# Attention and a gated recurrence on one core: the softmax division in the layout of the values product, context stores sent by ScalarE, low parts of x by GpSimd

## The chip, the cores and the metric

The kernel runs on one core of one Trainium2 chip. The metric is the device time of one execution in microseconds (us), lower is better. A core has TensorE (PE, matrix products), VectorE (DVE), ScalarE (ACT), GpSimd (POOL) and SyncE (SP, which only issues transfers), each with its own instruction stream; they wait for each other through semaphores.

## The reference

Sixteen sequences of 512 tokens with 256 features. Sliding-window attention with 16 heads of width 16, then a layernorm, then a recurrence over the sequences whose state feeds three gates, then a second layernorm.

```python
qkv = jnp.einsum('bse,fe->bsf', x, w_in)
scores = jnp.where(valid, qb @ k2.T * scale + slopes * delta, -jnp.inf)   # own block of 128 keys and the one before
out = softmax(scores) @ v2                                                 # per head, D = 16
x = layernorm(x + out @ w_out.T)                                           # attention half
ft, it = sigmoid(xt @ wf.T + c @ uf.T + bf), sigmoid(xt @ wi.T + c @ ui.T + bi)
gt = tanh(xt @ wc.T + c @ uc.T + bc)
c = ft * c + it * gt                                                       # scanned over the 16 sequences
h = tanh(x @ wo.T + c_final @ uo.T + bo)
x = layernorm(x + h)
```

## The kernel before

Every fp32 operand of a product is kept as a high and a low part ("hi" and "lo": the value rounded, and the rest), and each product is three passes over them (`PASSES`). ACT writes the high part with a Copy, DVE (or POOL) subtracts it for the low part.

The main loop has 16 iterations, and each engine has its own `iteration(t)` with its order written out by hand. One iteration is cut into 16 slots, `attend(0)` to `attend(15)`. In a slot PE computes raw scores of sequence t for two heads (`raw_scores`, L940), DVE takes their row maxima (`maxima`, L689), and PE computes the final scores of the slot seven places back (`scores`, L961), of which ACT takes the exponential (`exps`, L448) and POOL clears what lies outside the window (`window`, L347 and L349). A PSUM bank of raw scores is written again only when DVE has read it, one slot later (`red_done`), and one of final scores only when ACT has read it (`exp_done`). Between the slots stand the other products: of sequence t+1 the queries and keys (`project_qk`, `qk_halves`), of t the values (`v_halves`), of t-1 the product of probabilities and values (`values`, L975), of t-2 the output projection (`out_halves`), of t-3 and t-2 the gates (`gate_halves`). Halves of 64 rows run side by side under L921.

The path that the change touches: `values(t-1, g)` gives, for four heads, a bank with 32 rows per head: 16 rows of contexts, the denominator in row 16 (the value matrix has a column of ones), tokens along the free axis. ACT copies it to `ctx_raw` (`ctx_out`, L459), PE transposes it in four blocks (`ctx_transpose`, L983), DVE takes reciprocals of the denominators (L698) and multiplies them into `o_tok` (L703, both in `normalise`). In the next iteration PE transposes `o_tok` back in eight blocks (`o_transpose`, L1016), ACT and DVE make `oT`'s two parts (`ot_hi`, `ot_lo`), and `project_out` or `out_halves` multiplies by `Wout`. `x_hi` (ACT, L426) and `x_lo` (DVE, under L661, where a helper stands for all low parts) split the transposed input of the next sequence, from `xt_raw`. `update` (L736, L738, L740) makes the new state, and `c_hi`, `c_lo` (POOL, L364) split it.

SP issues transfers in one order: `parts_to_dram` and `stack` bring queries and keys through DRAM into stacked layout, `max_to_stack` adds the row of maxima, and the loads of `xt_raw` and `x_res` and the store of `y` lie between. After the loop `last_sequences` finishes the sequences in flight, and a second phase computes the tanh and the second layernorm for all sequences.

## Time and profile before

| | |
|---|---|
| time, three runs | 1002.41, 1003.2, 1004.5 us; median 1003.2 |
| profiled execution | 1004.63 us, of which its instructions span 1002.9 us |
| PE busy | 915.2 us, 91% of the span, 9500 matmuls |
| DVE busy | 719.0 us, 72% |
| ACT busy | 575.9 us, 57% |
| POOL busy | 407.6 us, 41% |
| granted TensorE clock, mean | 0.953 of full |
| DMA, main queue | 129.95 MB, 44.2% of 16 engines |

Busy means that an instruction was in execution; matmuls overlap each other, so a busy PE is an engine that issues without a gap, not one at its peak. An engine's idle time is named with what ended it. The span has a start until about 27 us, the 16 iterations, the last sequences from about 829 us, and the second phase from about 906 us.

### The profile page before, as it was taken

What the parts mean: (1) busy time and instruction counts of PE and PEld (TensorE: products, weight loads), DVE (VectorE), ACT (ScalarE), POOL (GpSimd) and SP (SyncE); (2) the same over time, 40 slices, a digit from 0 to 9 for tenths busy, and PEclk for the clock granted to TensorE, in tenths of its full rate; (3) what the DMA queues carried; (4) which work ended last, traced back from release to release, by engine and by line L of the source; (5) the groups of instructions that cost most, each with busy time, mean ns of one, the idle gap of its engine ahead of it and who ended that gap; (6) DMA issues with size and microseconds to landing.
All of it is one profiled execution on the core that took longest, in us unless ns stands there. A gap on an engine that the chain in (4) does not pass through costs nothing.

```text
span 1002.9 us, 25924 instructions
## 1 busy us (share of the span) xinstructions
PE 915.2 (91%) x9500; PEld 753.2 (75%) x9500; DVE 719.0 (72%) x2795; ACT 575.9 (57%) x1167; POOL 407.6 (41%) x687
## 2 busy tenths in 40 slices
PE   3587879999999999999999999999999989889994
PEld 2375668878788878788878787878787867668884
DVE  7766576877777777777777778787878673327885
ACT  5144556555656565656565656565756464325886
POOL 5142443354444444444444444444444353101443
PEclk9577889999999999999999999999999999899998
DMA  7634443535454545444544454444444400121764
GB/s 257 168 117 121 129 140 126 151 120 143 135 140 137 138 138 139 139 137 139 134 143 133 144 129 146 129 147 129 146 108 145 124 28 22 42 91 49 221 202 132
DMA packets 93534, 131.86 MB, mean 131 GB/s; under 512 B 12128, under 2 KB 47584, under 8 KB 93408
## 3 DMA queue, kind: packets, MB, share of 16 engines
q1 hardware_dynamic: 93136, 129.95, 44.2%
q8 instruction: 76, 1.25, 0.5%
q14 instruction: 50, 0.41, 0.1%
q10 hardware_dynamic: 272, 0.26, 0.1%
HBM read 79.31 MB, written 50.33 MB: 129 GB/s over the span
## 4 chain that ended last, share of the span: by engine, by line
PE 64%; DVE 25%; ACT 5%; issue 4%; POOL 2%; DMA 0%; ACTq 0%; DVEq 0%; POOLq 0%
PE bank L921 29%; DVE bank L689 11%; PE bank L909 11%; PE bank L940 8%; PE bank L975 7%; PE bank L961 3%; DVE max_q L689 3%; DVE qk_parts L661 2%; PE bank L983 2%; DVE gate L738 2%; DVE gate L736 1%; PE bank L1016 1%; PE bank L1029 1%; ACT Pt L643 1%; DVE stats L877 1%
## 5 line engine op out<-in xcount | busy, mean ns | idle before, releaser
L689 DVE CUSTOM_DVE_ANT_0 bank<-bank,mask 128x256 f32<-128x256 f32 (+1 forms) x1024 | 369.3, 423 | 136.1 <-PE bank L940 134.5
L448 ACT ACTIVATE Pt<-bank 128x512 f32<-128x512 f32 (+1 forms) x512 | 248.2, 536 | 204.1 <-PE bank L961 204.0
L347 POOL TENSOR_SCALAR_AFFINE_SELECT Pt<-Pt 128x512 f32<-128x512 f32 x256 | 174.7, 682 | 414.8 <-ACT Pt L448 414.8
L940 PE MATMUL bank<-Ks,Qs 59*128 59x256 f32 (+1 forms) x1024 | 149.5, 320 | 51.3 <-DVE max_q L689 40.5
L940 PEld LDWEIGHTS bank<-Ks,Qs 59*128 59x128 f32 x1024 | 108.5, 192 | 94.8 <-DVE max_q L689 54.5
L689 DVE DVE_READ_ACCUMULATOR2_ANT max_q<- 128x1 f32 x1024 | 144.6, 141 | 0.0
L349 POOL TENSOR_SCALAR_AFFINE_SELECT Pt<-Pt 128x384 f32<-128x384 f32 x256 | 139.3, 544 | 0.0
L975 PE MATMUL bank<-Pt,Vp 128*32 128x256 f32 (+1 forms) x2048 | 131.2, 377 | 0.0
L921 PE MATMUL bank<-x1T,Wg 64*128 64x512 f32 x960 | 128.0, 398 | 0.8 <-DVE o_tok L703 0.8
L921 PE MATMUL bank<-cT,Ug 64*128 64x512 f32 x960 | 125.8, 393 | 0.0
L961 PE MATMUL bank<-Qs,Ks 60*128 60x256 f32 (+1 forms) x1024 | 112.1, 271 | 0.4 <-ACT Pt L448 0.3
L975 PEld LDWEIGHTS bank<-Pt,Vp 128*32 128x32 f32 x2048 | 81.5, 116 | 32.1 <-issue 8.2
L921 PEld LDWEIGHTS bank<-cT,Ug 64*128 64x128 f32 x960 | 89.6, 184 | 17.7
L921 PEld LDWEIGHTS bank<-x1T,Wg 64*128 64x128 f32 x960 | 87.4, 185 | 18.6 <-DVE o_tok L703 0.9
L961 PEld LDWEIGHTS bank<-Qs,Ks 60*128 60x128 f32 x1024 | 95.7, 193 | 2.3 <-issue 1.3
L486 ACT ACTIVATE gate<-bank,bias_half 128x512 f32<-128x512 f32 x64 | 42.5, 687 | 44.7 <-PE bank L921 23.9
L459 ACT ACTIVATE ctx_raw<-bank 128x512 f32<-128x512 f32 x64 | 38.2, 597 | 49.7 <-PE bank L983 47.6
L909 PE MATMUL bank<-xT,Win 128*128 128x512 f32 x204 | 55.5, 425 | 8.6 <-DVE Win L661 8.6
L921 PE MATMUL bank<-Win,xT 64*128 64x256 f32 x768 | 56.7, 291 | 0.0
L909 PEld LDWEIGHTS bank<-xT,Win 128*128 128x128 f32 x204 | 40.5, 205 | 17.6 <-DVE Win L661 8.6
L921 PEld LDWEIGHTS bank<-Win,xT 64*128 64x128 f32 x768 | 52.8, 197 | 0.0
L661 DVE SCALAR_TENSOR_TENSOR qk_parts<-bank,qk_parts 128x512 fp32r<-128x512 f32 x64 | 42.6, 686 | 14.2 <-ACT qk_parts L431 14.2
(111 smaller groups left out, 1345.7 us busy)
## 6 DMA issues: line engine op xcount, KB each, us to landing
parts_dram<-qk_parts SPq DMA_DIRECT2D x128, 256.0 KB
Qs<-parts_dram SPq DMA_DIRECT2D x128, 128.0 KB, 2.6
Ks<-parts_dram SPq DMA_DIRECT2D x128, 128.0 KB, 2.7
xt_raw<-in_xt SPq DMA_DIRECT2D x16, 512.0 KB, 4.2
Qs<-parts_dram SPq DMA_DIRECT2D x128, 64.0 KB, 2.6
Ks<-parts_dram SPq DMA_DIRECT2D x128, 64.0 KB, 2.7
x_res<-in_x SPq DMA_DIRECT2D x16, 512.0 KB, 3.9
x_dram<-y SPq DMA_DIRECT2D x16, 512.0 KB, 3.7
```

Source lines behind the costliest of these rows:

```text
L347: gp.affine_select(out=p4[:, :, 0:128], in_=p4[:, :, 0:128], compare_op=ALU.is_ge, fill=0.0, base=0, pattern=[[0, 4], [1, 128]], channel_m ...
L349: gp.affine_select(out=p4[:, 0:3, 128:256], in_=p4[:, 0:3, 128:256], compare_op=ALU.is_ge, fill=0.0, base=0, pattern=[[0, 3], [-1, 128]], ...
L448: sc.activation(probabilities(g, 2 * pair + odd)[:, S * a:S * a + n], SC[odd][:, 0:n], ACT.Exp).then_inc(exp_done, 1)
L459: sc.activation(ctx_raw[:, :], bank[:, :], ACT.Copy).then_inc(ctx_done, 1)
L486: ins = sc.activation(gate[:, k if k == 3 else which, :], bank[:, :], ACT.Tanh, bias=bias_half[:, which, j:j + 1], scale=0.5)
L661: return ve.scalar_tensor_tensor(out_, in_, scale, hi.bitcast(F32), op0=ALU.mult, op1=ALU.subtract)
L689: ins = ve.tensor_tensor_reduce(out=raw, in0=raw, in1=mask[:, keys], scale=1.0, scalar=MASKED, op0=ALU.add, op1=ALU.max, accum_out=max_q[: ...
L909: ins = te.matmul(out_, w, m, start=(first and n == 0), stop=(last and n == len(todo) - 1))
L921: ins = te.matmul(out_, w(r), m(r), start=(turn == 0 and opens and n == 0), stop=final, skip_group_check=True)
L940: ins = te.matmul(MX[odd][:, 256 * (n % 2):256 * (n % 2) + 256][:, keys], Qs[rows, 2 * g + pair, n * WIN:(n + 1) * WIN], Ks[rows, 2 * g + ...
L961: ins = te.matmul(SC[odd][:, 256 * (j % 2):256 * (j % 2) + width], Ks[rows, 2 * g + pair, j * WIN:(j + 1) * WIN], Qs[rows, 2 * g + pair, j ...
L975: ins = te.matmul(bank[32 * hh:32 * hh + 32, j * WIN:j * WIN + width], Vp[:, j, PITCH * h:PITCH * h + 32], probabilities(g, hh)[:, 256 * j ...
```

## The change

The division by the softmax denominator moves. For sequences 0 to 14 ACT copies each values bank to `ctx_raw` as before, and then sends it itself to `ctx_dram` (one transfer of 256 KB for each g, four per sequence). SP loads the 256 context rows from there to `o_un`, already in the layout that `oT` needs, in two transfers (`load_contexts`), and the 16 denominator rows in pieces of 128 tokens to `den_q` (`load_denominators`, four transfers). DVE transposes them in blocks of 32 (`turn_denominators`), takes the reciprocal of 64 columns (`invert_denominators`) and transposes them back (`turn_inverses`). SP stores them to `inv_dram` (`store_inverses`) and loads them again with every row repeated for the 16 rows of its head (`spread_inverses`, two transfers of 256 KB). POOL multiplies (`scale_contexts`), and ACT and DVE split the result (`ot_hi`, `ot_lo`, now from SBUF). PE's transposes and DVE's `normalise` stay for the last sequence alone.

Besides: the low parts of x are POOL's from sequence 2 on, and their high parts are made two sequences ahead, in slots 11 and 12; `update` is cut in `forget` and `take_in`, and `forget` stands earlier; `stack(t, 2)` goes ahead of the load of `xt_raw`; `Wo` and `Uo` are no longer loaded and split at the start but in the last sequences (`load_last_weights`, `last_weights_hi`), into `Win`'s space.

```diff
-        Wo = sb("Wo", [128, 2, KC, E], F32R)
-        Uo = sb("Uo", [128, 2, KC, E], F32R)
...
+        o_un = sb("o_un", [128, KC, S])
+        inv_den = sb("inv_den", [128, KC, S])
+        den_q = sb("den_q", [128, 128])
+        den_t = sb("den_t", [128, 128])
+        last_o_tok = sb("last_o_tok", [128, NB, E])
...
+        Wo, Uo = Win[:, :, :, 0:E], Win[:, :, :, E:2 * E]
+        out_stage = xt_raw[:, :, :]
...
+        ctx_dram = nc.dram_tensor("ctx_dram", [2, QUADS, 128, S], F32).ap()
+        inv_dram = nc.dram_tensor("inv_dram", [2, 32, S], F32).ap()
...
+            def load_denominators(t):
+
+                sp.wait_ge(den_cleared, 1)
+                for g in range(QUADS):
+                    wait(sp, ctx_stored[g], 16, t, 16)
+                wait(sp, inv_stored, 16, t - 1, 16)
+                rows = ctx_dram[t % 2].rearrange("g (h r) (q i) -> q (g h) r i", r=2 * D, i=128)[:, :, D, :]
+                for q in range(4):
+                    sp.dma_start(den_q[32 * q:32 * q + H, :], rows[q]).then_inc(den_in, 16)
+
+            def load_contexts(t, c):
+                for g in (2 * c, 2 * c + 1):
+                    wait(sp, ctx_stored[g], 16, t, 16)
+                wait(sp, otlo_done, 2, t - 1, c + 1)
+                rows = ctx_dram[t % 2, 2 * c:2 * c + 2].rearrange("g (h r) s -> (g h) r s", r=2 * D)[:, 0:D, :]
+                sp.dma_start(o_un[:, c, :], rows).then_inc(o_un_in[c], 16)
+
+            def store_inverses(t):
+                wait(sp, inv_turned, 1, t, 1)
+                sp.dma_start(inv_dram[t % 2].rearrange("r (q i) -> q r i", i=128), den_q[:, :]).then_inc(inv_stored, 16)
+
+            def spread_inverses(t):
+
+                wait(sp, inv_stored, 16, t, 16)
+                for c in range(KC):
+                    wait(sp, scaled_done, 2, t - 1, c + 1)
+                    rows = inv_dram[t % 2, 8 * c:8 * c + 8]
+                    sp.dma_start(inv_den[:, c, :], rows.unsqueeze(1).to_broadcast([8, D, S])).then_inc(inv_in[c], 16)
+
+            def load_last_weights():
+
+                sp.wait_ge(xlo_done, 2 * B)
+                for n, w in enumerate((w_o, u_o)):
+                    sp.dma_start(out_stage[:, n, :].rearrange("p (c n) -> p c n", c=KC), w.rearrange(v, p=128)).then_inc(last_weights_in, 16)
...
+                if now: stack(t, 2)
+                if by_rows: load_contexts(t - 1, 0)
                 if real(t + 2): load_xt(t + 2)
                 if now:
-                    stack(t, 2)
...
                 if n1: stack(t + 1, 0)
+                if by_rows:
+                    load_denominators(t - 1)
+                    load_contexts(t - 1, 1)
                 if now: max_to_stack(t, 2)
                 if n1: parts_to_dram(t + 1, 1)
+                if by_rows:
+                    store_inverses(t - 1)
+                    spread_inverses(t - 1)
+                if t == B - 1: load_last_weights()
...
+            def x_lo(t, c):
+                wait(pool, xhi_done, 2, t, c + 1)
+                gp.tensor_tensor(xT[:, t % 2, 1, c, :], xt_raw[:, c, :], xT[:, t % 2, 0, c, :].bitcast(F32), ALU.subtract).then_inc(xlo_done, 1)
+
+            def scale_contexts(t, c):
+
+                wait(pool, o_un_in[c], 16, t, 16)
+                wait(pool, inv_in[c], 16, t, 16)
+                gp.tensor_tensor(o_un[:, c, :], o_un[:, c, :], inv_den[:, c, :], ALU.mult).then_inc(scaled_done, 1)
...
+                if p2 and t - 2 < B - 1:
+                    for c in range(KC):
+                        scale_contexts(t - 2, c)
...
+                    if real(t + 2):
+                        for c in range(KC):
+                            x_lo(t + 2, c)
...
-                wait(act, ct_ready, 4, t, g)
+                pt, pg = before(t, g)
+                if pt < B - 1:
+                    wait(act, ctx_stored[pg], 16, pt, 16)
+                else:
+                    act.wait_ge(ct_ready, g)
                 sc.activation(ctx_raw[:, :], bank[:, :], ACT.Copy).then_inc(ctx_done, 1)
-
-            def ot_hi(t, c, bank):
+                if t < B - 1:
+                    wait(act, ctx_done, 4, t, g + 1)
+                    sc.dma_start(ctx_dram[t % 2, g], ctx_raw[:, :]).then_inc(ctx_stored[g], 16)
+
+            def ot_hi(t, c):
                 if c == 0:
                     wait(act, op_ready, 2, t - 1, 2)
-                wait(act, ot_ready, 2, t, c + 1)
+                wait(act, scaled_done, 2, t, c + 1)
+                sc.activation(oT[:, 0, c, :], o_un[:, c, :], ACT.Copy).then_inc(othi_done, 1)
...
+            def last_weights_hi():
+
+                act.wait_ge(last_weights_in, 32)
+                act.wait_ge(v_ready, 2 * B)
+                sc.activation(out_stage[:, 1, :], out_stage[:, 1, :], ACT.Copy, scale=0.5).then_inc(u_o_halved, 1)
+                sc.activation(Wo[:, 0, :, :], out_stage[:, 0, :].rearrange("p (c n) -> p c n", c=KC), ACT.Copy).then_inc(last_hi, 1)
...
-                    ot_hi(t - 2, 0, B0)
-                    ot_hi(t - 2, 1, B1)
-                attend(1)
-                if n1: x_hi(t + 1, 0)
+                    ot_hi(t - 2, 0)
+                    ot_hi(t - 2, 1)
                 attend(2)
-                if n1: x_hi(t + 1, 1)
+                if t == 0: x_hi(1, 1)
...
                 v_out(t, 0, A0)
+                if real(t + 2): x_hi(t + 2, 0)
                 attend(12)
                 v_out(t, 1, A1)
+                if real(t + 2): x_hi(t + 2, 1)
...
+                last_weights_hi()
                 c_hi(t - 2, 0)
...
-            act.wait_ge(weights_in, 80)
-            for n in range(5):
+            act.wait_ge(weights_in, 48)
+            for n in range(3):
...
+            def turn_denominators(t):
+
+                wait(dve, den_in, 64, t, 64)
+                ve.transpose(den_t[:, :], den_q[:, :]).then_inc(den_turned, 1)
+
+            def invert_denominators(t):
+                wait(dve, den_turned, 1, t, 1)
+                own = den_t[:, :].rearrange("p (b r) -> p b r", r=32)[:, :, 0:H]
+                ve.reciprocal(own, own).then_inc(den_inverted, 1)
+
+            def turn_inverses(t):
+                wait(dve, den_inverted, 1, t, 1)
+                ve.transpose(den_q[:, :], den_t[:, :]).then_inc(inv_turned, 1)
+
+            def ot_lo(t, c):
+                wait(dve, othi_done, 2, t, c + 1)
+                minus_hi(oT[:, 1, c, :], o_un[:, c, :], oT[:, 0, c, :]).then_inc(otlo_done, 1)
+
...
-                if p1: normalise(t - 1, 0, A0)
+                if p3: forget(t - 3, 0)
+                attend(1)
+                if t == 0: x_lo(1, 0)
+                attend(2)
+                if t == 0: x_lo(1, 1)
                 if p2:
-                    ot_lo(t - 2, 0, B0)
-                    ot_lo(t - 2, 1, B1)
-                attend(1)
-                if n1: x_lo(t + 1, 0)
-                attend(2)
-                if n1: x_lo(t + 1, 1)
...
-                if p1: normalise(t - 1, 3, A0)
-                if p2:
-                    x1_lo(t - 2, 0, B0)
-                    x1_lo(t - 2, 1, B1)
+                if p1: turn_denominators(t - 1)
+                if p2: x1_lo(t - 2, 0, B0)
+                if p1: invert_denominators(t - 1)
+                if p2: x1_lo(t - 2, 1, B1)
+                if p1: turn_inverses(t - 1)
...
-                    wait(pe, maxrow_done, 4, t - 1, 4)
-                    ctx_transpose(t - 1, 0, A0)
-                if p2:
-                    wait(pe, gate_done, 6, t - 3, 1)
-                    o_transpose(t - 2, 0, B0)
-                    freed(pe, (gate_done, 6, t - 3, 2), (ctx_done, 4, t - 1, 1))
...
-                    wait(pe, o_done, 4, t - 1, 1)
+                    wait(pe, maxrow_done, 4, t - 1, 4)
...
                     o0, o1 = out_halves(0, B0), out_halves(1, B1)
+                    freed(pe, (gate_done, 6, t - 3, 1), (maxrow_done, 4, t - 1, 3))
+                    freed(pe, (gate_done, 6, t - 3, 2), (ctx_done, 4, t - 1, 1))
                     wait(pe, otlo_done, 2, t - 2, 2)
...
-                    wait(pe, maxrow_done, 4, t, 1)
-                    ctx_transpose(t - 1, 1, A0)```

What stands in PE's order behind `values(t-1, 1)` at the start of an iteration, before. L1016 is `o_transpose`, L940 and L961 are slot 1.

```order
L975 MATMUL bank<-Pt,Vp 32x256 x12
L975 MATMUL bank<-Pt,Vp 32x128 x4
L983 MATMUL bank<-ident,ctx_raw 128x128 x4
L1016 MATMUL bank<-ident,o_tok 128x128 x8
L940 MATMUL bank<-Ks,Qs 128x256 x4
L961 MATMUL bank<-Qs,Ks 128x256 x4
L921 MATMUL bank<-x1T,Wg 128x512 x12
```

The same place in the changed kernel (L1106 is `values`, L1071 and L1092 the raw and the final scores):

```order
L1106 MATMUL bank<-Pt,Vp 32x256 x12
L1106 MATMUL bank<-Pt,Vp 32x128 x4
L1071 MATMUL bank<-Ks,Qs 128x256 x4
L1092 MATMUL bank<-Qs,Ks 128x256 x4
L1052 MATMUL bank<-x1T,Wg 128x512 x12
```

The twelve transposes between the values product and slot 1 are gone, and nothing takes their place on PE.

ACT's order in slots 12 to 14, before, from the copy of the first half of the values of sequence t (L438, `v_out`) to the exponentials of slot 14 (L448), with `qk_hi` (L431), `ctx_out` (L459) and `x1_hi` (L477) between:

```order
L438 ACTIVATE Vp<-bank 128x2x16x16
L448 ACTIVATE Pt<-bank 128x384 x2
L438 ACTIVATE Vp<-bank 128x2x16x16
L431 ACTIVATE qk_parts<-bank 128x512
L454 ACTIVATE max_rows<-bank 16x128
L448 ACTIVATE Pt<-bank 128x512 x2
L431 ACTIVATE qk_parts<-bank 128x512
L459 ACTIVATE ctx_raw<-bank 128x512
L477 ACTIVATE x1T<-bank 128x512 x2
L448 ACTIVATE Pt<-bank 128x384 x2
```

And in the changed kernel (L517 is `v_out`, L505 `x_hi`, L527 `exps`, L510 `qk_hi`, L542 and L545 `ctx_out` and its transfer, L578 `x1_hi`):

```order
L517 ACTIVATE Vp<-bank 128x2x16x16
L505 ACTIVATE xT<-xt_raw 128x512
L527 ACTIVATE Pt<-bank 128x384 x2
L517 ACTIVATE Vp<-bank 128x2x16x16
L505 ACTIVATE xT<-xt_raw 128x512
L510 ACTIVATE qk_parts<-bank 128x512
L533 ACTIVATE max_rows<-bank 16x128
L527 ACTIVATE Pt<-bank 128x512 x2
L510 ACTIVATE qk_parts<-bank 128x512
L542 ACTIVATE ctx_raw<-bank 128x512
L545 DMA ctx_dram<-ctx_raw 128x512
L578 ACTIVATE x1T<-bank 128x512 x2
```

The two high parts of x stand between the copies and `qk_hi` now, and a transfer stands between `ctx_out` and `x1_hi`.

SP's order at an iteration's end, before: the last rows of `stack(t+1, 0)`, then `max_to_stack(t, 2)`, `parts_to_dram(t+1, 1)` and, of the next iteration, `max_to_stack(t, 3)` and the first of `stack(t+1, 1)`.

```order
L254 DMA Ks<-parts_dram 32x2x512
L262 DMA Qs<-max_rows 1x8x128 x2
L239 DMA parts_dram<-qk_parts 8x16x512 x4
L262 DMA Qs<-max_rows 1x8x128 x2
L254 DMA Qs<-parts_dram 32x2x512
```

And in the changed kernel:

```order
L267 DMA Ks<-parts_dram 32x2x512
L286 DMA den_q<-ctx_dram 16x128 x4
L293 DMA o_un<-ctx_dram 128x1x512
L275 DMA Qs<-max_rows 1x8x128 x2
L252 DMA parts_dram<-qk_parts 8x16x512 x4
L297 DMA inv_dram<-den_q 4x32x128
L305 DMA inv_den<-inv_dram 128x1x512 x2
L275 DMA Qs<-max_rows 1x8x128 x2
L267 DMA Qs<-parts_dram 32x2x512
```

Eight transfers came in, and the last three of them wait for DVE and for a store to land, ahead of `max_to_stack` and `stack` of the next iteration.

## Rows read from the trace of the kernel before

**Rows 1.** The page: the chain that ended last, by engine.

```profile
PE 64%; DVE 25%; ACT 5%; issue 4%; POOL 2%; DMA 0%; ACTq 0%; DVEq 0%; POOLq 0%
```

**Rows 2.** Windows: us, busy of PE, PEld, DVE, ACT, POOL, clock, DMA, GB/s.

```profile
127.00:178.00 51.00, 46.33 (x500) 37.45 (x501) 36.44 (x165) 28.32 (x59) 19.42 (x36) 0.90 0.45 135
431.00:482.00 51.00, 49.96 (x580) 41.67 (x578) 39.50 (x167) 31.44 (x65) 22.73 (x38) 1.00 0.47 137
```

**Rows 3.** Timeline of PE, one iteration: start, us; idle before in brackets.

```profile
425.20 0.39 PE L940 MATMUL bank<-Ks,Qs 59*128 59x128 f32 x4
...
427.54 0.66 PE L983 MATMUL bank<-ident,ctx_raw 128*128 128x128 f32 x4
428.04 1.04 PE L1016 MATMUL bank<-ident,o_tok 128*128 128x128 f32 x8
429.00 0.50 PE L940 MATMUL bank<-Ks,Qs 59*128 59x256 f32 x4
...
436.31 1.58 PE L921 MATMUL bank<-Wout,oT 64*128 64x256 f32 x24
...
442.43 0.66 PE L983 MATMUL bank<-ident,ctx_raw 128*128 128x128 f32 x4
442.84 3.02 PE L909 MATMUL bank<-xT,Win 128*128 128x512 f32 x12
...
454.78 0.66 PE L983 MATMUL bank<-ident,ctx_raw 128*128 128x128 f32 x4
455.37 0.50 PE L940 MATMUL bank<-Ks,Qs 59*128 59x256 f32 x4
...
458.04 0.32 PE L940 MATMUL bank<-Ks,Qs 59*128 59x128 f32 x1 [0.50 <-DVE max_q L689]
458.80 0.49 PE L940 MATMUL bank<-Ks,Qs 59*128 59x128 f32 x3 [0.44 <-DVE max_q L689]
...
467.29 0.66 PE L983 MATMUL bank<-ident,ctx_raw 128*128 128x128 f32 x4
467.78 1.35 PE L1029 MATMUL bank<-ident,y 128*128 128x128 f32 x8
...
475.70 0.41 PE L940 MATMUL bank<-Ks,Qs 59*128 59x128 f32 x4
```

**Rows 4.** Groups by line: busy us, mean ns | idle before, releaser.

```profile
L364 POOL TENSOR_TENSOR cT<-c,cT 128x512 fp32r<-128x512 f32 x26 | 32.7, 1275 | 0.0
...
L703 DVE TENSOR_TENSOR o_tok<-bank,rden 128x256 f32<-128x256 f32 x64 | 27.2, 425 | 12.0 <-PE bank L1016 10.3
...
L661 DVE SCALAR_TENSOR_TENSOR xT<-xt_raw,xT 128x512 fp32r<-128x512 f32 x32 | 23.3, 730 | 7.1 <-ACT xT L426 6.9
...
L698 DVE RECIPROCAL rden<-bank 128x16 f32<-128x16 f32 x64 | 15.9, 248 | 42.6 <-PE bank L983 42.6
```

**Rows 5.** Timeline of ACT at slot 12 of that iteration.

```profile
465.01 0.60 ACT L431 ACTIVATE qk_parts<-bank 128x512 fp32r<-128x512 f32 x1 [0.16 <-PE bank L921]
```

**Rows 6.** Timeline of the start: ACT's transfer, DVE, POOL.

```profile
0.79 0.47 ACTq L600 DMA_DIRECT2D Pt<-in_w_in  x1
...
24.78 5.57 DVE L661 SCALAR_TENSOR_TENSOR cT<-c,cT 128x512 fp32r<-128x512 f32 x2 [1.16 <-ACT cT L613]
...
28.09 1.71 POOL L340 TENSOR_TENSOR Uo<-ctx_raw,Uo 128x512 fp32r<-128x512 f32 x1
...
30.27 0.29 DVE L689 CUSTOM_DVE_ANT_0 bank<-bank,mask 128x128 f32<-128x128 f32 x1
```

**Rows 7.** DMAs from or to `parts_dram` by tile: time to landing.

```profile
DMA to landing us min/median/max: 2.0/2.7/5.1
```

**Rows 8.** Timeline of SP's queue at an iteration's end.

```profile
467.65 3.33 SPq L239 DMA_DIRECT2D parts_dram<-qk_parts  x4
```

**Rows 9.** Timeline of PE in the last sequences; the wait for a layernorm.

```profile
857.25 1.94 PE L1029 MATMUL bank<-ident,y 128*128 128x128 f32 x8 [3.99 <-ACT y L470]
```

**Rows 10.** Groups by line: one high part of a weight, on ACT.

```profile
L416 ACT ACTIVATE Uo<-ctx_raw 128x512 fp32r<-128x512 f32 x1 | 0.6, 631 | 0.0
```

More of the change, by code:

```diff
@@ L776, in iteration @@
                     qk_lo(t + 1, 1, B1)
+                if p3: forget(t - 3, 1)
                 attend(7)
[L778 removed]
+                if p3: take_in(t - 3, 0)
                 attend(8)
[L780 to L781 removed]
+                if p3: take_in(t - 3, 1)
                 attend(9)
@@ L798, in last_sequences @@
                 (A0, A1), (B0, B1) = pairs_of(B)
-                normalise(t, 0, A0)
-                ot_lo(t - 1, 0, B0)
-                ot_lo(t - 1, 1, B1)
+                last_normalise(0, A0)
+                ot_lo(t - 1, 0)
+                ot_lo(t - 1, 1)
                 residual(t - 1, 0, B0)
@@ L814, in last_sequences @@
                 x1_lo(t - 1, 1, B1)
-                normalise(t, 3, MX[0])
+                last_normalise(3, MX[0])
                 update(t - 1, 0)
-                ot_lo(t, 0, MX[0])
-                ot_lo(t, 1, MX[1])
+                last_ot_lo(0, MX[0])
+                last_ot_lo(1, MX[1])
                 update(t - 1, 1)
@@ L978, in values, with last_ctx_transpose @@
                 ins.then_inc(pv_ready, 1)
-            def ctx_transpose(t, g, bank):
-                wait(pe, ctx_done, 4, t, g + 1)
+            def last_ctx_transpose(g, bank):
+                wait(pe, ctx_done, 4, B - 1, g + 1)
                 for n in range(NB):
@@ L1011, in project_qk, with last_o_transpose @@
                                      for c in range(KC)], qk_ready)
-            def o_transpose(t, c, bank):
-                wait(pe, o_done, 4, t, 4)
+            def last_o_transpose(c, bank):
+                pe.wait_ge(o_done, 4)
                 for n in range(NB):
-                    ins = te.transpose(bank[:, WIN * n:WIN * (n + 1)], o_tok[:, n, 128 * c:128 * c + 128], ident[:, :])
+                    ins = te.transpose(bank[:, WIN * n:WIN * (n + 1)], last_o_tok[:, n, 128 * c:128 * c + 128], ident[:, :])
                 ins.then_inc(ot_ready, 1)
```

143 lines of the change are left out of this document (79 added, 64 removed).

## The prediction

> **What bounds the kernel now.** I read the chain that ended last first: 64% of it is PE and 25% DVE [rows 1]. Then the windows by stage: in the steady part PE is busy 49.96 us of 51 at the full clock, DVE 39.50, ACT 31.44, POOL 22.73, and the DMA engines 0.47 [rows 2]. So there PE issues almost without a gap, and every instruction taken from its stream should shorten the iteration. Two sequences in, from 127 to 178 us, PE is busy 46.33 of 51 [rows 2]; the rest are waits for DVE's maxima. Last I read PE's timeline of one whole iteration, from 425.20 to 475.70, so 50.50 us [rows 3]. Its two idle times over 0.25 us, 0.50 and 0.44, end with DVE's maxima in slot 10 [rows 3].
>
> **What is removed from PE.** A matmul's own length (0.27 to 0.4 us) is no price, since matmuls overlap; the step from the first of a group to the next group is. The transposes of `ctx_raw` at 427.54 take 0.50 until `o_transpose` starts, `o_transpose` 0.96 until slot 1, and the other three groups 0.41, 0.59 and 0.49 [rows 3]. Sum 2.95 us per iteration. Nothing comes in on PE.
>
> **What leaves DVE, and where it waits.** Four `normalise` at 0.248 + 0.425 = 0.67 us are 2.7 us, two low parts of x at 0.73 are 1.5 [rows 4]. In slots 7 to 10, where PE waited 0.94 us for it, DVE loses one `normalise` and has both `forget` instructions earlier (0.7 each, by the row of the same size [rows 4]): 2.0 us less work against 0.59 us less on PE before it. I take the whole 0.94 as gained; the bounds are 0 and 0.94. With it the iteration could fall by 3.89 us.
>
> **What comes in on DVE.** Two block transposes of 128 columns and a reciprocal of 64 columns stand in no trace of before. A transpose costs between 0.248 (16 columns) and 0.73 (512 columns) [rows 4]; I take 0.35, since 128 columns are nearer the first. The Trainium skill (VectorE: DVE Perf Modes, The three transpose paths) gives 311 ns for 128x128 in bf16; by it the sum would be the same. The reciprocal lies between 0.248 and four times that, 0.99; I take 0.6. Together 1.3 us (0.75 to 2.45), in slot 13, where DVE waits for the high parts of x1 anyway. Cover gone, they would delay the maxima of slot 14.
>
> **What comes in on ACT, and the give-back in slots 12 to 15.** ACT has idle time enough in sum, but `qk_hi` of slot 12 waited only 0.16 us for PE [rows 5], and two high parts of x, 0.63 us each by the row of one of the same size [rows 10], now stand ahead of it. Behind it wait DVE's low part, then the maxima of slot 13, then the second low part, then the bank into which PE transposes x1. The delay is between 0 and 1.26 - 0.16 = 1.10; I take 0.6, since the exponentials between had some idle time of their own. The transfer that ACT issues behind `ctx_out` costs its queue 0.47 us [rows 6], four times an iteration; in slot 13 it stands ahead of the high parts of x1, for which PE's gates wait: 0 to 0.47, I take 0.3. At slots 1, 5 and 10 PE arrives 1.5 us or more earlier at a bank that ACT or DVE must first empty: I take 0.4 for all (0 to 0.8). Given back: 1.3 us (0 to 2.4).
>
> **POOL.** Two low parts of x and two scalings at 1.275 us [rows 4] make its 22.7 us 27.8 of about 48. `values(t, 0)` and `values(t-1, 2)` wait for its windows; both have more than 1.5 us of room by my reckoning, so 0.
>
> **The long path.** From the end of slot 13's low parts: DVE's three instructions and the two low parts of x1 between them, 1.3 + 1.4 us; a store; when it has landed, two loads; two scalings, 2.55; ACT's and DVE's parts, in their places behind slots 1 and 2. A transfer takes 2.0 to 5.1 us to land, median 2.7 [rows 7]. PE has its x1 transposes 42.6 us after the iteration's start [rows 3], which becomes about 40; so the inverses leave DVE at about 43, land in DRAM at 45.7, are spread at 48.9, which is 1.0 us into the next iteration (period 47.9), and are multiplied in at 3.6. ACT takes them at 4.6 to 5.9 and DVE at 7.8 to 9.1. PE's output projection stands 11.11 us into the iteration [rows 3], 9.65 when 1.46 us are gone. Up to ACT's step there is room of about 3.5 us. SP is free in time: `parts_to_dram` holds it for 3.33 us [rows 8] until about 42.5.
>
> **Start and end.** The first maximum is at 30.27, right behind two DVE low parts that took 5.57 us beside POOL's low parts of weights, the last of which is `Uo`'s, 1.71 us until 29.80 [rows 6]. Two of POOL's five low parts and three of ACT's high parts go. I take 2.3 us (0 to 3.4, twice 1.71). At the end ACT makes three high parts of 0.63 us [rows 10] just ahead of the layernorm for which PE waits 3.99 us already [rows 9]: 1.9 us lost. Eight transposes, 0.96 [rows 3], go from PE there, but they hid a `normalise`; I take 0.6. Net loss 1.3.
>
> **The sum.** Iterations 3 to 15: 13 times (3.89 - 1.3 = 2.6), 33.8 us. Iterations 1 and 2: PE idle 4.7 us of 51 [rows 2], DVE relieved by 4.2 - 1.3 and PE by 3 or less; I take 4.2 each (2.6 to 6), 8.4. Start 2.3, end -1.3. In all 43.2. The profiled execution took 1004.6 us for a span of 1002.9; it becomes 959.7 and 961.4. The median of the three runs stands 1.4 lower, at 1003.2, so 960.
>
> **The rivals.**
> (a) Nothing is given back: 3.89 an iteration, and 943. For it: PE was the only engine without idle time. Against it: the 0.16 us of ACT.
> (b) POOL and DVE hold each other up. The two DVE low parts of 5.57 us for 2, against 0.73 for one elsewhere, ran beside POOL's two-input work [rows 4, 6]: such a pair costs DVE about 2 us more each. Four more POOL instructions of 1.275 us come in, and `ot_lo` now reads two SBUF operands, `forget` too. If two of these pairs an iteration fall on DVE instructions that PE waits for, at 1.0 us each, the gain falls by 2 us an iteration: 986. Against it: most DVE work reads PSUM, and DVE idles 11.5 us of 51 [rows 2]. The Trainium skill (SBUF — State Buffer, Who interferes with whom) says that a VectorE instruction with two SBUF inputs and a GpSimd instruction that reads SBUF exclude each other for the whole instruction; by that rule, the trace at 24.78 us agrees.
> (c) The long path comes late and PE stops in slot 3. Both hops at the longest landing, 5.1 twice instead of 2.7 twice, eat 4.8 us against 3.5 of room: 1.3 late, 13 times, 977.
> (d) The same, and slower than before: at 43.2 / 13 = 3.3 us of lateness an iteration nothing is left, which needs hops of 12 us for the two. Then SP, which sits in that wait, also brings `stack` late. At 4 us late: 1012. Against it: the longest landing is 5.1 [rows 7]; for it: 2.1 MB more per iteration (four stores and four loads of 256 KB) on top of 6.9 (137 GB/s [rows 2] over 50.5 us), small rows, and SP's order is full.
> (e) The bound passes wholly to ACT or DVE at once and the time stays: 1003. I see no row for it, as both are idle for a fifth of the time or more.
>
> **How the numbers follow.** Likeliest, 943 to 978 (gains of 3.9 to 1.6 us an iteration, with the ends' bounds; (a) and (c) are its edges): 0.68. Better than 943: 0.04. (b), 978 to 994: 0.13. A late path short of undoing the gain, 994 to 1001: 0.04. (e): 0.02. (d): 0.09. The range 944 to 990 leaves out not quite 2 in 10. Faster by over 0.2%, about what a measurement tells here, 0.89; within it 0.02; slower 0.09.
>
> **What would show it.** Period of iterations from 50.5 to about 47.9; PE without L983 and L1016 rows until the last sequences; no wait of over 0.3 us of PE for DVE in slot 10; new short waits of PE in slots 12 to 14, with DVE's low parts waiting for ACT's `qk_hi`; `scale_contexts` ending about 4 us into an iteration; PE's wait for the layernorm near the end at about 5.9. Wrong would be: a wait of PE at the output projection, which would be the long path; DVE's `ot_lo`, `forget` or transposes of over 1 us each, which would be (b); a period under 47.

## The result

Four runs of the changed kernel took 1042.02, 1044.45, 1050.46 and 1051.42 us, median 1047.45; four of the kernel before on the same chip 1003.85. The ratio is 1.043, with a 95% interval of 1.037 to 1.049. It is slower, where 960 was forecast. The profiled execution took 1042.02 us for a span of 1040.3.

The page of the profile after gives busy time by engine:

```profile
PE 895.3 (86%) x9140; PEld 742.6 (71%) x9140; DVE 684.8 (66%) x2693; ACT 576.1 (55%) x1167; POOL 479.9 (46%) x745
```

PE has 360 matmuls less and DVE 34 us less work, as planned, and yet the span grew by 37.4 us. The windows of the stages of [rows 2], after (same columns):

```profile
127.00:178.00 51.00, 41.43 (x451) 32.94 (x448) 31.84 (x143) 26.70 (x56) 24.52 (x40) 0.83 0.75 174
431.00:482.00 51.00, 47.76 (x545) 40.31 (x537) 36.28 (x156) 30.57 (x64) 27.18 (x43) 0.97 0.66 179
```

No engine has taken PE's place: PE, DVE and ACT idle more in both stretches, and POOL, the one with more work, is busy for only about half of them. That is the mark of waits in a ring of engines and not of a new bound. The view of waits names them (who waited, for what: us in total, times, longest):

```profile
POOL o_un L432 <- DMA inv_den<-inv_dram: 173.8, 30, 11.4
ACT oT L551 <- POOL o_un L432: 88.1, 29, 4.4
...
PE bank L1092 <- ACT Pt L527: 41.2, 15, 5.6
```

Read from the bottom: PE stops once in every sequence for an exponential of ACT (L527), because its bank of scores isn't read yet. ACT is not busy then; it stands in `ot_hi` (L551) for GpSimd's product, and GpSimd stands for the spread of the inverses. The timeline of one such passage starts on SP's queue (start, us to issue, what, how many):

```profile
539.26 4.80 SPq L252 DMA_DIRECT2D parts_dram<-qk_parts  x4
544.11 1.44 SPq L297 DMA_DIRECT2D inv_dram<-den_q  x1
550.33 1.29 SPq L305 DMA_DIRECT2D inv_den<-inv_dram  x2
551.66 0.68 SPq L275 DMA_DIRECT2D Qs<-max_rows  x1
```

VectorE's last transpose of the inverses began at 541.41 and took 0.30, but SP was issuing `parts_to_dram` until 544.06. The store of 64 KB then took until 550.33 to land, 6.2 us, read from the issue of the spread, for which SP waits until the store has landed. All that time SP stood still, the row maxima behind it too. GpSimd, ACT and PE in the same passage (in brackets the idle time before, and what ended it):

```profile
554.28 1.29 POOL L432 TENSOR_TENSOR o_un<-o_un,inv_den 128x512 f32<-128x512 f32 x1 [10.77 <-DMA inv_den<-inv_dram]
```
```profile
555.66 0.63 ACT L551 ACTIVATE oT<-o_un 128x512 fp32r<-128x512 f32 x1 [4.37 <-POOL o_un L432]
558.17 0.63 ACT L551 ACTIVATE oT<-o_un 128x512 fp32r<-128x512 f32 x1 [1.88 <-POOL o_un L432]
558.71 0.85 ACT L527 ACTIVATE Pt<-bank 128x384 f32<-128x384 f32 x2
```
```profile
559.33 0.79 PE L1092 MATMUL bank<-Qs,Ks 60*128 60x256 f32 x4 [2.81 <-ACT Pt L527]
559.89 1.68 PE L1052 MATMUL bank<-Wout,oT 64*128 64x256 f32 x24
```

The exponentials of slot 2 are ready work, queued behind `ot_hi`. From the end of VectorE's transpose to the first multiplication lie 12.6 us.

One iteration later the wait is longer, and it costs twice, in idle time and in clock. PE's timeline, then its windows (stretch, length, busy, granted clock, DMA share, GB/s):

```profile
613.14 1.08 PE L1092 MATMUL bank<-Qs,Ks 60*128 60x256 f32 x4 [4.35 <-ACT Pt L527]
613.81 2.97 PE L1052 MATMUL bank<-Wout,oT 64*128 64x256 f32 x24
```
```profile
607.00:611.00 4.00, 1.79 (x18) 1.00 1.07 144
611.00:615.00 4.00, 1.86 (x15) 0.71 1.10 185
615.00:619.00 4.00, 4.00 (x42) 0.50 1.12 150
619.00:623.00 4.00, 3.89 (x56) 0.94 0.83 161
```

After 4.35 us of idleness the granted clock is at 0.50, the 1.2 GHz level, and the same 24 matmuls that took 1.68 us above take 2.97.

### The profile page after: what moved, and what is told of

Its sections match the earlier page's. It is cut to its first block and busy times, and to the rows that moved or that the text cites. A ratio compares the mean times of both kernels' runs of the same rounds, so it can differ in the third digit from the quotient of the medians.

```text
span 1040.3 us, 25344 instructions
## 1 busy us (share of the span) xinstructions
PE 895.3 (86%) x9140; PEld 742.6 (71%) x9140; DVE 684.8 (66%) x2693; ACT 576.1 (55%) x1167; POOL 479.9 (46%) x745
## 5 line engine op out<-in xcount | busy, mean ns | idle before, releaser
L527 ACT ACTIVATE Pt<-bank 128x512 f32<-128x512 f32 (+1 forms) x512 | 248.0, 536 | 166.2 <-PE bank L1092 164.8
L1071 PE MATMUL bank<-Ks,Qs 59*128 59x256 f32 (+1 forms) x1024 | 145.7, 322 | 45.8 <-DVE max_q L793 28.0
L1071 PEld LDWEIGHTS bank<-Ks,Qs 59*128 59x128 f32 x1024 | 109.6, 199 | 83.9 <-DVE max_q L793 36.9
L1092 PE MATMUL bank<-Qs,Ks 60*128 60x256 f32 (+1 forms) x1024 | 120.2, 285 | 48.1 <-ACT Pt L527 41.2
L1092 PEld LDWEIGHTS bank<-Qs,Ks 60*128 60x128 f32 x1024 | 99.5, 200 | 56.3 <-issue 42.7
L1106 PE MATMUL bank<-Pt,Vp 128*32 128x256 f32 (+1 forms) x2048 | 131.7, 378 | 0.0
L1052 PE MATMUL bank<-x1T,Wg 64*128 64x512 f32 x960 | 128.6, 398 | 2.3 <-ACT ctx_raw L542 2.3
L1052 PE MATMUL bank<-cT,Ug 64*128 64x512 f32 x960 | 126.7, 393 | 0.0
L432 POOL TENSOR_TENSOR o_un<-o_un,inv_den 128x512 f32<-128x512 f32 x30 | 40.0, 1333 | 173.8 <-DMA inv_den<-inv_dram 173.8
L1106 PEld LDWEIGHTS bank<-Pt,Vp 128*32 128x32 f32 x2048 | 81.6, 116 | 32.2 <-issue 8.2
L1052 PEld LDWEIGHTS bank<-x1T,Wg 64*128 64x128 f32 x960 | 91.8, 185 | 17.4 <-issue 4.7
L1052 PEld LDWEIGHTS bank<-cT,Ug 64*128 64x128 f32 x960 | 94.5, 185 | 13.0
L551 ACT ACTIVATE oT<-o_un 128x512 fp32r<-128x512 f32 x30 | 18.9, 631 | 88.1 <-POOL o_un L432 88.1
L1052 PE MATMUL bank<-Wout,oT 64*128 64x256 f32 x672 | 61.7, 337 | 0.0
L765 DVE SCALAR_TENSOR_TENSOR oT<-o_un,oT 128x512 fp32r<-128x512 f32 x30 | 25.1, 836 | 51.0 <-ACT oT L551 50.8
L1052 PEld LDWEIGHTS bank<-Wout,oT 64*128 64x128 f32 x672 | 57.4, 244 | 0.0
```

What stands on the lines that cost most here:

```text
L432: gp.tensor_tensor(o_un[:, c, :], o_un[:, c, :], inv_den[:, c, :], ALU.mult).then_inc(scaled_done, 1)
L527: sc.activation(probabilities(g, 2 * pair + odd)[:, S * a:S * a + n], SC[odd][:, 0:n], ACT.Exp).then_inc(exp_done, 1)
L765: return ve.scalar_tensor_tensor(out_, in_, scale, hi.bitcast(F32), op0=ALU.mult, op1=ALU.subtract)
L1052: ins = te.matmul(out_, w(r), m(r), start=(turn == 0 and opens and n == 0), stop=final, skip_group_check=True)
L1071: ins = te.matmul(MX[odd][:, 256 * (n % 2):256 * (n % 2) + 256][:, keys], Qs[rows, 2 * g + pair, n * WIN:(n + 1) * WIN], Ks[rows, 2 * g + ...
L1092: ins = te.matmul(SC[odd][:, 256 * (j % 2):256 * (j % 2) + width], Ks[rows, 2 * g + pair, j * WIN:(j + 1) * WIN], Qs[rows, 2 * g + pair, j ...
```

## The experiments

The two theories. **The late path**: the inverses' two hops through DRAM end too late, and ready work stands behind the waits for them. **Traffic**: 2.1 MB more an iteration slow every transfer that PE's operands come by. Times of the kernel before were 1003 to 1005 us in every set.

### The division left out

```
 SP:   load_denominators, store_inverses, spread_inverses removed
 POOL: scale_contexts removed
 DVE:  turn_denominators, invert_denominators, turn_inverses removed
-                wait(act, scaled_done, 2, t, c + 1)
+                wait(act, o_un_in[c], 16, t, 16)
```

> The changed kernel with the division of sequences 0 to 14 left out (no denominators read, no transposes and reciprocal on VectorE, no store and spread of the inverses, no scaling on GpSimd); the contexts still go through DRAM and the high part waits for their load alone. Theory 1 (the path of the inverses is late, and ScalarE, GpSimd and SyncE stand waiting for it): the waits of PE for the exponentials (1 to 5.6 us an iteration) go, periods of 48 to 49 us, 955 to 975 us in all. Theory 2 (the 2 MB more of traffic an iteration slow every transfer): three quarters of that traffic are still there, so 1020 us or more.

Measured 978.64 us, ratio 0.976 (0.974 to 0.977), 4 us above the range of theory 1 and far from that of theory 2. Of PE's waits for an exponential one of 0.6 us is left in its view of waits. Traffic is refuted as the main cause: three quarters of it are in this kernel. PE's windows over the 13 sequences from the fourth on, of the kernel before, of the changed one and of this one:

```profile
171.00:829.00 658.00, 640.60 (x7404) 0.99 0.46 131
```
```profile
175.00:864.00 689.00, 624.43 (x7091) 0.97 0.67 167
```
```profile
171.00:804.00 633.00, 604.04 (x7100) 0.99 0.62 169
```

Here PE's busy time falls by 36.6 us against before, 2.8 a sequence, near the 2.95 of the prediction. In the changed kernel it fell by 16.2 only, and PE idled 64.6 us instead of 17.4. So of the 56 us between the last two windows, 35.6 are more idle time and 20.4 are the same matmuls taking longer. The rows show one cause of these, the clock: a mean of 0.97 over 689 us, with 1 and 0.5 as the levels, is some 41 us at the low one, which loses half of them; 0.99 over 633 us is 13. By this estimate the clock accounts for some 14 of the 20.4, with an error of several us, since the column has two digits. It isn't the only thing that changes the busy time: the kernel with the direct way, further down, has 0.99 too and 9.5 us more of it than this one, for which no run shows a cause.

### The transfers alone, in the kernel before

```
+                if t < B - 1:
+                    wait(act, ctx_done, 4, t, g + 1)
+                    sc.dma_start(ctx_dram[t % 2, g], ctx_raw[:, :]).then_inc(ctx_stored[g], 16)
 SP:   the loads, the store and the spreads at the changed kernel's places, into tiles nobody reads;
       the store doesn't wait for DVE, and the spread reads the inverses stored an iteration earlier
```

> The kernel before (division in the context transposes, as it was) with the last weights loaded late to make room, and with the changed kernel's transfers added at the same places in the queues, their data read by nobody: four context stores by ScalarE, two context loads, four denominator loads, the inverse store and two spreads an iteration. Theory 1: nothing waits for them, so 1000 to 1012 us. Theory 2: 1025 us or more, with Qs and Ks landing in 3.5 us instead of 2.6.

Measured 1012.35 us, ratio 1.008 (1.006 to 1.011), at the upper edge of theory 1. So the traffic costs something, and with the late weights it is worth 9 us and not 44: an iteration of the steady part takes 50.9 us instead of 50.5. What this kernel lacks is SP's wait for DVE and for the store of the same iteration. The landings of transfers from or to `parts_dram` rose from 2.0/2.7/5.1 [rows 7] to 2.1/3.0/7.5, yet PE waited only 5 us more for keys in all (15.1 against 10.0) and 2.6 for row maxima.

### The inverses ahead of the parts

```
+                if by_rows:
+                    store_inverses(t - 1)
+                    spread_inverses(t - 1)
                 if n1: parts_to_dram(t + 1, 1)
-                if by_rows:
-                    store_inverses(t - 1)
-                    spread_inverses(t - 1)
```

> The changed kernel with the store of the inverses and their spread issued by SyncE ahead of the 1 MB of projection parts instead of behind it; all work is kept. Theory 1 with the queue as the cause of the lateness: the store issues at once, lands about 2.5 to 3 us later instead of 6.2, the spread lands some 6 us earlier, and the waits of PE for the exponentials go: 970 to 1000 us. Theory 2 (traffic): the same bytes, so 1035 to 1050. If the parts, now later, are waited for by the stacks instead, it stays above 1003 with PE waiting on the loads of Qs and Ks.

Measured 1030.43 us, ratio 1.028 (1.024 to 1.031). SP's queue, and PE's waits:

```profile
529.79 0.56 SPq L297 DMA_DIRECT2D inv_dram<-den_q  x1
532.37 1.27 SPq L305 DMA_DIRECT2D inv_den<-inv_dram  x2
533.76 4.35 SPq L252 DMA_DIRECT2D parts_dram<-qk_parts  x4
538.15 3.59 SPq L275 DMA_DIRECT2D Qs<-max_rows  x2
```
```profile
PE bank L1092 <- DMA Qs<-max_rows: 31.7, 24, 3.2
...
PE bank L1071 <- DMA Ks<-parts_dram: 27.3, 14, 10.9
```

The store now lands in 2.6 us instead of 6.2, and of PE's waits for an exponential one of 0.6 us is left. But SP waits for VectorE and for the store ahead of the parts, and then row maxima and keys come late. Of the 27.3 us for keys, 10.9 are one wait at the start, where the kernel before has one of 10.0. The third outcome named in the expectation came true, and the forecast of 970 to 1000 did not: the lateness had only changed its place.

### Store and spread by ScalarE's queue

```
                 attend(14)
+                if p1: store_inverses(t - 1)
                 attend(15)
+                if p1: spread_inverses(t - 1)
```

> The changed kernel with the store and the spread of the inverses issued by ScalarE, on its own DMA queue (store after slot 14, spread after slot 15), so that SyncE waits for neither and the store isn't behind the 1 MB of parts. With the store in front on SyncE's queue the waits of PE only moved from the exponentials to the loads of row maxima and keys (1030 us). Theory 1, refined (it is the in-order wait for the store, wherever it stands, that costs): both waits go, 978 to 992 us, close to the 979 without any division. If ScalarE's own wait for the store and its 2.5 us of issues hold the gates and exponentials back: 995 to 1015. If traffic or the clock is what is left: above 1020.

Measured 1046.95 us, ratio 1.042 (1.037 to 1.048): no gain at all. The expectation had a time above 1020 for the case that traffic or the clock is what is left; the rows show late hops and waits for them. SP first, then ACT, then PE's wait for the exponentials:

```profile
542.16 4.46 SPq L252 DMA_DIRECT2D parts_dram<-qk_parts  x4
```
```profile
545.65 0.57 ACTq L540 DMA_DIRECT2D inv_dram<-den_q  x1
...
552.89 1.22 ACTq L548 DMA_DIRECT2D inv_den<-inv_dram  x2
554.21 1.26 ACT L584 ACTIVATE gate<-bank,bias_half 128x512 f32<-128x512 f32 x2 [5.32 <-issue]
```
```profile
PE bank L1091 <- ACT Pt L512: 39.6, 15, 4.8
```

The store took 7.2 us, though it wasn't on SP's queue. In the run above it took 2.6, and there too ScalarE had sent a context store of 256 KB 3.0 us before it; what that run lacked was the 1 MB of parts handed over at the same time. So leaving SP's queue doesn't make the store early. What the two late stores share is the parts on the DMA engines, which both queues use. The Trainium skill (DMA: Bandwidth & Descriptors, Issuing engines are not separate DMA queues) says this: transfers run on the same 16 DMA engines and interleave, whichever engine started them. These rows agree. And now ACT stood 5.32 us in front of its gates, so that PE still waited for exponentials, 39.6 us against 41.2 in the changed kernel.

### The way shortened and begun earlier

ScalarE sends each quad's four rows of denominators straight from `ctx_raw` into `den_q`, in which the flat order makes 16 partitions of 128 of them. VectorE inverts all 64 partitions at once. The store is then of 32 KB and no longer of 64, since the unused rows of `den_q` fall away. SP stores behind `stack(t + 1, 0)` and spreads ahead of the parts. All work is kept.

```
+                    sc.dma_start(den_q[16 * g:16 * g + 16, :], ctx_raw[D:128:2 * D, :]).then_inc(den_in, 16)
                     sc.dma_start(ctx_dram[t % 2, g], ctx_raw[:, :]).then_inc(ctx_stored[g], 16)
...
+                ve.reciprocal(den_t[0:64, :], den_q[0:64, :]).then_inc(den_inverted, 1)
...
                 if n1: stack(t + 1, 0)
                 if by_rows:
-                    load_denominators(t - 1)
+                    store_inverses(t - 1)
                     load_contexts(t - 1, 1)
                 if now: max_to_stack(t, 2)
+                if by_rows: spread_inverses(t - 1)
                 if n1: parts_to_dram(t + 1, 1)
```

> The changed kernel, all work kept, with a shorter way for the inverses that starts earlier: ScalarE sends each quad's four rows of denominators straight from its SBUF tile to the tile of denominators (one small transfer beside each context store), VectorE inverts them in one operation of 64 partitions behind slot 11 (no transposes), and SyncE stores and spreads them ahead of the 1 MB of parts. So far: a store ahead of the parts lands in 2.5 us, one behind them in 6.6 us on either queue, and what costs is that PE's work waits for it. Theory: the spread lands before slot 15, nobody waits for it, and the time comes down to that of the kernel without a division (979 us) plus 0 to 10: 975 to 990. Rival (the traffic and issues themselves): 1010 or more. Rival (SyncE delayed by 3 us ahead of the parts, as in the run with the inverses first): 1000 to 1025, with PE waiting on row maxima and keys.

Measured 985.35 us, ratio 0.981 (0.980 to 0.983): faster than both kernels, 1.9% faster than the one before, and inside the range of the theory. SP's queue, and GpSimd's two multiplications:

```profile
503.73 0.51 SPq L297 DMA_DIRECT2D inv_dram<-den_t  x1
504.35 0.65 SPq L293 DMA_DIRECT2D o_un<-ctx_dram  x1
506.01 1.30 SPq L275 DMA_DIRECT2D Qs<-max_rows  x2
507.42 1.32 SPq L305 DMA_DIRECT2D inv_den<-inv_dram  x2
508.85 5.31 SPq L252 DMA_DIRECT2D parts_dram<-qk_parts  x4
```
```profile
512.76 1.29 POOL L430 TENSOR_TENSOR o_un<-o_un,inv_den 128x512 f32<-128x512 f32 x1
514.85 1.30 POOL L430 TENSOR_TENSOR o_un<-o_un,inv_den 128x512 f32<-128x512 f32 x1 [0.80 <-DMA inv_den<-inv_dram]
```

SP does 1.95 us of other issues while the store lands, in a median of 2.3 us. The spread isn't as quick: its second half, issued at about 508.1 with the parts right behind it, still held GpSimd until 514.85, 6.7 us later and in slot 15. It did no harm, since GpSimd's scaling was still done at about the start of the next iteration: its waits for the spread fell from 173.8 us to 6.5, and PE's for an exponential from 41.2 to 1.6. PE's window of the same 13 sequences is 636 us long:

```profile
172.00:808.00 636.00, 613.55 (x7090) 0.99 0.64 181
```

### The same, with the store behind the parts again

Against the run above, the store and the spread are taken from their two places and stand behind the parts:

```
                 if n1: parts_to_dram(t + 1, 1)
+                if by_rows:
+                    store_inverses(t - 1)
+                    spread_inverses(t - 1)
```

> The kernel with the direct way for the denominators (985 us) with one thing put back: SyncE stores and spreads the inverses behind the 1 MB of projection parts, as the changed kernel does; the inversion on VectorE stays early. Theory (a store behind the parts lands in 6 to 7 us, its spread 3.7 us later, and the exponentials and the row maxima stand behind those two waits): 1025 to 1047 us, with PE waiting for the exponentials again. Rival (the early inversion was the gain): 980 to 1000.

Measured 1032.33 us (1021.53 to 1041.97), ratio 1.032 (1.025 to 1.038), inside the range of the theory. Moving three transfers back costs 47 us by the medians, while the direct way and the early inversion with the old place gain 15 against the changed kernel. SP's queue, and PE's wait for the exponentials, in the quickest of these executions:

```profile
531.95 4.12 SPq L252 DMA_DIRECT2D parts_dram<-qk_parts  x4
536.12 1.85 SPq L297 DMA_DIRECT2D inv_dram<-den_t  x1
542.08 1.29 SPq L305 DMA_DIRECT2D inv_den<-inv_dram  x2
```
```profile
PE bank L1084 <- ACT Pt L525: 22.1, 15, 5.9
```

The store of 32 KB takes 6.0 us to land here, in a median of 6.1 over its 15 landings, against 2.3 in the run above. Only the place of these three transfers in SP's order differs. So this pair shows that the place makes the store late, and what a late store costs with SP's wait for it.

### ScalarE's high parts two slots later

In the changed kernel `ot_hi` stands ahead of the exponentials of slot 2, and `ot_lo` ahead of slot 3's maxima. Here `ot_hi` stands behind the exponentials of slots 2 and 3, and `ot_lo` behind slot 3's maxima. ScalarE's part of the edit:

```
+                attend(2)
+                if t == 0: x_hi(1, 1)
+                attend(3)
                 if p2:
                     ot_hi(t - 2, 0)
                     ot_hi(t - 2, 1)
-                attend(2)
-                if t == 0: x_hi(1, 1)
-                attend(3)
```

> The changed kernel with ScalarE's high parts of the contexts two slots later, behind the exponentials of slots 2 and 3, and VectorE's low parts behind slot 3. The inverses come as late as before. Theory (late inverses cost by whatever stands behind the wait): the wait for the exponentials goes, but PE waits at the output projection instead, and the row maxima still stand behind SyncE's wait for the store: 1020 to 1045. Rival (the place of the high parts on ScalarE is the fault): 985 to 1000.

Measured 1083.67 us, ratio 1.078 (1.072 to 1.083), worse than either theory said. PE's waits:

```profile
PE bank L1052 <- DVE oT L765: 53.5, 14, 4.2
...
PE bank L1092 <- DMA Qs<-max_rows: 23.0, 18, 3.7
```

The wait went to the output projection, as expected, and grew; of the waits for an exponential 0.6 us is left, and those for row maxima went from 6.6 us to 23.0. Together these waits are 29 us longer than in the changed kernel; no run shows why. The place on ScalarE is not the fault.

### Moving the parts of x, and what it gives back

Three kernels. Without the division, the high parts of x moved from slots 11 and 12 to behind slot 14, GpSimd's low parts to the end of its iteration:

> The kernel without the division of sequences 0 to 14 (979 us), and ScalarE's high parts of x moved from slots 11 and 12 to behind slot 14, where ScalarE waits 2.5 us, GpSimd's low parts of x to the end of its iteration. This tests the term given back in slots 12 to 15. Theory: PE's wait for the queries' low part at the transposes of x1 (0.96 us an iteration, 15 iterations) goes, and 979 becomes 962 to 968. Rival: the wait is the shorter work's own (PE 3 us earlier, ScalarE and VectorE as late as before) and stays: 976 to 980.

Measured 971.72 us, ratio 0.967 (0.965 to 0.969). The division of sequences 0 to 14 is left out here too. The gain was 7 us and not 11 to 17, so the time lies between the ranges of the two theories. PE's waits for the queries' low part fell from 11.3 us in 13 times to 7.0 and not to nothing. But the profiled execution took 979.07 us, more than the other four (969.61 to 972.99), so this row doesn't show where the 7 us come from.

The same with the direct way and the whole computation:

> The same, and the high parts of x behind slot 14, which took 979 to 972 us without a division. Theory: 968 to 982 us, below the other by 4 to 10.

Measured 984.39 us, ratio 0.980 (0.978 to 0.982), which can't be told from the 985.35 without it and misses the range, though PE's waits for the queries' low part fell here too, from 8.9 us to 6.5. So the gain of 7 us above was not had a second time. The same with ScalarE's queue for the inverses:

> Both edits with all work kept: the inverses' store and spread on ScalarE's queue, the parts of x behind slot 14. Theory: the two gains add, 965 to 980 us. Rival: behind slot 14 the store's issue and the two high parts (together 2.7 us) now hold the exponentials of slot 15 and the gates, 985 to 1000.

Measured 1047.71 us, ratio 1.045 (1.039 to 1.051): as slow as ScalarE's queue alone, so neither outcome.

### One part of the change alone, in the kernel before

> The kernel before with one part of the change alone: high parts of x two sequences ahead, in slots 11 and 12 of ScalarE, low parts by GpSimd. VectorE loses two operations of 0.69 us. Theory of the prediction: VectorE's lateness at slot 10 shrinks, but qk_hi comes later in slot 12, so 995 to 1004 us. Rival (the ports that GpSimd and VectorE share): VectorE's long operations stretch, 1005 to 1015.

Measured 1003.83 us, ratio 1.000 (0.999 to 1.001). Relieving VectorE of these two operations is worth nothing by itself: PE's waits for its maxima are 38.2 us in all against 40.5, and 12 new waits of up to 0.5 us for `qk_lo`, 4.2 in all, take that back. GpSimd's added work beside VectorE's does no harm worth naming either: VectorE's low parts of queries and keys took 687 ns against 686, its maxima of 256 columns 460 against 459.

### A run that told little

The product was written into a tile nobody reads, and GpSimd made it later; so the output lacks the division.

> The changed kernel with every transfer and every operation of the division kept, but its product written into the tile of inverses, which nobody reads, and GpSimd doing it after the masks of slots 0 to 8; the high part reads the undivided contexts as soon as they are loaded. So the softmax division has no effect on the output. Theory 1: ScalarE and GpSimd no longer wait for the spread, 960 to 990 us. Theory 2: all bytes are there, 1035 to 1050. Near 1015: half of it is SyncE's own wait for the store, which delays the row maxima.

Measured 1182.74 us, ratio 1.182 (1.177 to 1.187). I had given SP's load of the contexts a wait for that later product, and SP, which does everything in order, stood in it:

```profile
PE bank L1093 <- DMA Qs<-max_rows: 151.8, 27, 10.2
```

It doesn't part the two theories. It does show once more what a wait in SP's order can cost.

## Why the prediction was wrong

**The step that failed** is the long path's: "so the inverses leave DVE at about 43, land in DRAM at 45.7, are spread at 48.9", with "room of about 3.5 us", and "SP is free in time". The inverses left VectorE 5.0 us before the iteration's end (541.71 against 546.70), where 4.9 was said. From there on it went otherwise. SP was not free in time. By [rows 8] it ended the parts at 470.98, that is 45.8 us into an iteration of 50.5, so about 43.2 in one of 47.9, and not 42.5. In the changed kernel it began them 7.4 us before the iteration's end, behind five transfers for the contexts and denominators that take 2.3 us to issue (535.02 to 537.49), and issued them for 4.80 us instead of 3.33. So the store was 2.4 us late in issue. It then took 6.2 us to land, and the spread 3.95. That is 12.6 us against 5.9. I took the landing of 2.7 us from the median of the transfers from and to `parts_dram` of the kernel before, wherever they stood; the same store landed in 2.6 us ahead of the parts and in 6.2 behind them.

**The rival that came true was (d)**, which needed "hops of 12 us for the two" and had 0.09; the two hops alone took 10.2, and 12.6 with the wait for the issue. Its mechanism was right, its price was not: it gave 1012 for 4 us late, and by the same rule the 6.7 us beyond the plan, less the 3.5 of room, would give some 1002; 1047 came. What was missing is who stands behind each wait. I looked for PE's stop at the output projection. It came just ahead of that, at the final scores of slot 3, because exponentials that were ready stood behind `ot_hi` on ScalarE, and the row maxima behind SP's wait. Idle stretches also brought the clock down, which I had not counted at all: of PE's longer busy time, 20.4 us over 13 sequences, some 14 by the estimate above.

**The other rivals.** (a), nothing given back, and (c), a path 1.3 us late, didn't come: the first falls with the 0.96 us below, the second with the 12.6 above. Nor did (e), a time that stays.

**PE's transposes, 2.95 an iteration**: about right, 2.8 by PE's busy time in the kernel without a division, though 2.1 in the one with the direct way. **Slot 10, 0.94 gained**: half right. The wait of 0.50 went, the one of 0.44 stayed.

**Given back in slots 12 to 15, 0.6 for `qk_hi`**: too low, but inside its bounds. The 0.16 us that `qk_hi` had waited [rows 5] were gone, and PE's timeline shows in slot 13:

```profile
539.48 0.66 PE L1160 MATMUL bank<-ident,y 128*128 128x128 f32 x4 [0.96 <-DVE qk_parts L765]
```

**New operations on VectorE**, from the groups by line (mean ns behind the busy time):

```profile
L432 POOL TENSOR_TENSOR o_un<-o_un,inv_den 128x512 f32<-128x512 f32 x30 | 40.0, 1333 | 173.8 <-DMA inv_den<-inv_dram 173.8
...
L765 DVE SCALAR_TENSOR_TENSOR oT<-o_un,oT 128x512 fp32r<-128x512 f32 x30 | 25.1, 836 | 51.0 <-ACT oT L551 50.8
...
L805 DVE RECIPROCAL den_t<-den_t 128x64 f32<-128x64 f32 x15 | 8.2, 544 | 0.0
...
L800 DVE STREAM_TRANSPOSE den_t<-den_q 128x128 f32<-128x128 f32 x15 | 4.5, 302 | 0.0
```

0.35 and 0.6 were taken, 0.30 and 0.54 came. Rival (b) would have shown in the second line: with two SBUF operands the low part took 836 ns in the mean (685 to 1739) against 686 from PSUM, so it was longer at times, by 0.15 us in the mean and not 1.0.

**The start**: the first maximum came at 28.08 instead of 30.27 [rows 6], 2.2 us earlier where 2.3 was said. It brought nothing: the last transposes of maxima of sequence 0 came 1.0 us later than before, and PE waited for keys ahead of them:

```profile
39.28 0.80 PE L1071 MATMUL bank<-Ks,Qs 59*128 59x128 f32 x4 [4.62 <-DMA Ks<-parts_dram]
```

**The end**: PE waited 5.55 us for the layernorm against 3.99 [rows 9], 1.6 more where 1.9 was said.

**The sum**, had the path been hidden: 43.2 us were forecast, and the kernel without a division gained 24.5 and the one with the direct way 19.3, so both lie in the range that was given. By the sequences' last transposes of maxima in PE's timeline, the kernel without a division lost 2.1 us until the first (2.3 gain forecast), gained 1.8 in the next two (8.4), 25.5 in thirteen (33.8) and lost 1.4 at the end (1.3). So 960 would have been missed in any case, by the terms of the start, of the first iterations, of slot 10 and of what ScalarE gives back, and by a wait that the prediction did not have: 8.6 us of PE for row maxima, in seven times. What the direct way still loses against no division, 7 us, stays open: the traffic of the spread, the operations of VectorE and GpSimd and ScalarE's additional transfers were not tried apart.

## What to carry to other kernels

When work goes from a bound engine to a way through DRAM, don't price a hop by the median landing of the trace: ask what is handed to the DMA engines just ahead of it, and put small transfers that others wait for in front of large ones that are needed later. Here that was worth 47 us (1032 against 985). Then go along every in-order queue that waits for the hop, and write down the ready work behind it, for that is what the lateness costs. A wait put on the queue engine holds transfers of other stages (1030 us with the store in front and SP waiting for it); give it other issues to do until the hop has landed, and begin the hop earlier.

## What the hardware showed that I had not expected

- A 64 KB store landed in 2.6 us ahead of 1 MB of stores, in 6.2 behind them on the same queue, and in 7.2 from another engine's queue with the parts in flight. One of 32 KB landed in a median of 2.3 us ahead of them and 6.1 behind them, so half the bytes didn't help.
- The granted clock went to 0.50 after an idle time of 4.35 us of PE, but stayed at 1.00 after one of 2.81; 24 matmuls of the output projection took 2.97 us at the low level and 1.68 at the high one.
- A third more traffic (182 GB/s in the stretch from 431 to 482 us against 137 [rows 2]) cost a kernel whose PE is busy 98% of that stretch 0.8%, with no engine waiting for what it carried.
- One DMA carried 4 partitions of 512 words to 16 of 128, so that no engine had to change the layout, and a reciprocal of 64 partitions by 128 took 0.94 us, less than the 1.14 of two transposes and a reciprocal of half the columns.
